# A fused dilation, state-space and convolution kernel: the scans begin with zero, ScalarE puts the kept state into their input, the extras sit in other slots

## The reference

```python
x = x + _L0_conv_ref(_gn(x))                 # 3x3 dilation (maximum)
x = x + _L1_conv_ref(_gn(x), ...)            # Mamba block on 4x4 patches
x = x + _L2_conv_ref(_gn(x), weight, bias)   # 3x3 convolution
x = x + _L3_conv_ref(_gn(x), weight, bias)   # 3x3 convolution

def step(h, inputs):                         # inside the Mamba block, token by token
    dt_t, x_t, B_t, C_t = inputs
    h = h * jnp.exp(dt_t[..., None] * A) + (dt_t * x_t)[..., None] * B_t[:, None, :]
    y = jnp.einsum('bds,bs->bd', h, C_t)
    return (h, y)
...
y = (ys + xc * D) * jax.nn.silu(z)
return jnp.einsum('bld,ed->ble', y, out_proj_w)
```

## Time and profile before

| | |
|---|---|
| three runs | 15040.47, 15045.57, 15050.49 us (median 15045.57) |
| the profiled execution | 15054.33 us, of which the span is 15052.5 us |
| busy, of the span | DVE 93%, POOL 90%, PE 84%, ACT 60% |
| scans (VectorE) | 8774.5 us with `carry`, 1202.5 us with 0.0 |
| products hc (GpSimd) | 9604.5 us |
| decays (ScalarE) | 5569.3 us |
| granted TensorE clock, mean | 0.949 |

### The profile page before, as it was taken

The page is one execution under the profiler, slowest core; times in us unless marked ns, Lnnn a source line. Parts: engine busy times, 40 slices in busy tenths (PEclk is TensorE's granted clock), DMA queues, the critical chain, the costliest instruction groups (busy, mean ns, idle before and its releaser), DMA issues.

```text
span 15052.5 us, 162697 instructions
## 1 busy us (share of the span) xinstructions
PE 12595.5 (84%) x27626; PEld 4973.4 (33%) x27626; DVE 13978.7 (93%) x12371; ACT 8975.3 (60%) x16239; POOL 13580.6 (90%) x6103
## 2 busy tenths in 40 slices
PE   4888888888888888888888888888888888888887
PEld 1333333333333333333333333333333333333332
DVE  5999999999999999999999999999999999999995
ACT  3556665566665666665656665666656666666563
POOL 5999999999999999999999999999999999999995
PEclk9999999999999999999999999999999999999998
DMA  3343443434434344443444434344343444434442
GB/s 93 105 118 116 111 123 104 125 108 112 123 106 127 106 111 121 111 124 104 113 121 110 123 106 121 113 112 122 105 129 105 109 123 111 122 107 113 121 109 81
DMA packets 1258399, 1701.57 MB, mean 113 GB/s; under 512 B 402204, under 2 KB 551140, under 8 KB 1257124
## 3 DMA queue, kind: packets, MB, share of 16 engines
q1 hardware_dynamic: 1257220, 1689.56, 40.4%
HBM read 1525.54 MB, written 124.13 MB: 110 GB/s over the span
## 4 chain that ended last, share of the span: by engine, by line
PE 33%; DVE 29%; issue 21%; POOL 9%; ACT 4%; DVEq 1%; DMA 1%; SPq 1%; POOLq 0%; ACTq 0%
PE y_ps L1026 18%; DVE h L1192 16%; DVE u_in L1176 10%; POOL hc L659 7%; PE side_ps L1037 2%; PE side_ps L1041 2%; PE b_ps L1077 2%; PE proj_ps L980 2%; POOL u_in L636 2%; PE y_ps L1023 2%; PE proj_ps L1002 2%; PE side_ps L1012 1%; PE side_ps L1045 1%; DVE vmax L1155 1%; DVE stats L1124 1%
## 5 line engine op out<-in xcount | busy, mean ns | idle before, releaser
L659 POOL TENSOR_TENSOR hc<-h,c_sb 128x1024 f32<-128x1024 f32 x4096 | 9604.5, 2358 | 952.5 <-DVE h L1192 816.6
L1192 DVE TENSOR_TENSOR_SCAN h<-a_ps,carry,u_in 128x512 f32<-128x512 f32 x7168 | 8774.5, 1264 | 367.0 <-ACT a_ps L792 196.1
L1026 PE MATMUL y_ps<-hc,ident 128*128 128x512 f32 x16400 | 8183.7, 629 | 446.3 <-POOL hc L659 440.0
L792 ACT ACTIVATE a_ps<-dt,a_neg 128x512 f32<-128x512 f32 x8192 | 5569.3, 688 | 4634.2 <-DVE h L1192 4604.4
L1026 PEld LDWEIGHTS y_ps<-hc,ident 128*128 128x128 f32 x16400 | 3191.3, 200 | 3985.2 <-issue 3065.3
L1176 DVE TENSOR_TENSOR u_in<-dtx,b_ps 128x1024 f32<-128x1024 f32 x2816 | 3368.2, 1196 | 228.0 <-PE b_ps L1077 186.4
L636 POOL TENSOR_TENSOR u_in<-dtx,b_sb 128x1024 f32<-128x1024 f32 x1281 | 3020.9, 2358 | 0.1
L1077 PE MATMUL b_ps<-b_parts,select 96*128 96x512 bf16 x2816 | 1123.9, 399 | 1639.7 <-DVE u_in L1176 1594.1
L1077 PEld LDWEIGHTS b_ps<-b_parts,select 96*128 96x128 bf16 x2816 | 278.5, 99 | 3169.7 <-DVE u_in L1176 2599.2
L1192 DVE TENSOR_TENSOR_SCAN h<-a_ps,u_in 128x512 f32<-128x512 f32 x1024 | 1202.5, 1204 | 69.0 <-POOL hc L659 55.8
L980 PE MATMUL proj_ps<-u_ln,w_x 128*128 128x512 f32 x2064 | 971.8, 593 | 4.6 <-ACT u_ln L744 3.7
(11 more groups left out here) (100 smaller groups left out, 7224.3 us busy)
## 6 DMA issues: line engine op xcount, KB each, us to landing
c_sb<-bc_dram SPq DMA_DIRECT2D x4100, 256.0 KB, 3.2
b_sb<-bc_dram SPq DMA_DIRECT2D x1283, 256.0 KB, 3.2
raw<-x SPq DMA_DIRECT2D x68, 512.0 KB
x_dram<-vmax SPq DMA_DIRECT2D x68, 512.0 KB, 4.6
z<-x_dram SPq DMA_DIRECT2D x68, 512.0 KB, 8.8
out<-raw SPq DMA_DIRECT2D x272, 128.0 KB
x_dram<-x SPq DMA_DIRECT2D x129, 256.0 KB, 4.0
x<-x_dram SPq DMA_DIRECT2D x136, 224.0 KB, 8.3
```

Of the source, the lines that this page charges most:

```text
L659: pool.tensor_tensor(hc[:, ring_at(c * S + s, HC_RING)], h[:, ring_at(c * S + s, H_RING)], c_sb[:, s // C_GROUP % C_RING, s % C_GROUP:s % ...
L792: act.activation(a_ps[:, a_slot(c * S + s, half)], dt[:, c % 2, half], ACT.Exp, scale=a_neg[:, at:at + 1]).then_inc(a_made, 1)
L1026: mm = pe.matmul(y_ps[:, half], ident[:, :], hc[:, ring_at((c * S + s) % (NC * S), HC_RING), half], start=False, stop=(s == S - 1), skip_g ...
L1192: dve.tensor_tensor_scan(h[:, r, half], a_ps[:, a_slot(c * S + s, half)], u_in[:, s % U_RING, half], start, ALU.mult, ALU.add).then_inc(h_ ...
```

## The change

1. **Scans.** All scans start with 0.0. In chunks 1 to 7 ScalarE adds the kept state's share to column 0 of the input instead: u[:, 0] += first_a * carry, one ACTIVATE on 128 x 1 for each half (`add_carry`), after the step's first decay and before its second. `first_a` is the decay of column 0 for all 32 states, made once a chunk (two ACTIVATEs of 128 x 32). The scan of such a step now waits for `carried` instead of for the input itself.
2. **Products two states ahead.** VectorE makes the input of state s + 2 at step s (before: s + 1), and TensorE broadcasts B for s + 1 at step s.
3. **GpSimd's states.** `POOL_U` keeps ten states: 22 and 25 leave, 0 and 24 come.
4. **Convolutions in five parts** in steps of their own; the strided residual product and the edge product are apart.
5. **Other slots**: the third product of the output projection 5 to 8, its copy (`residual`) 5 to 7, the store of x2 6 to 8 and with it the loads of z 7..10 to 9..12, `COPY_X` (6, 9) to (7, 10), `SILU` 13 to 14, `BASE` 10 to 12, the first softplus pieces (20, 22) to (21, 23), and two group-norm pieces by one step.

```diff
-POOL_U = [2, 6, 9, 11, 14, 17, 19, 22, 25, 27]
+POOL_U = [0, 2, 6, 9, 11, 14, 17, 19, 24, 27]
...
-CENTER, VAR, OUT = 0, 3, 5
+CENTER, VAR, OUT = 0, 3, (5, 5, 8)
...
-COPY_X, COPY_Z, SILU = (6, 9), (11, 13), 13
-GATE, STORE_X2, BASE = 2, OUT + 1, 10
+COPY_X, COPY_Z, SILU, RESIDUAL = (7, 10), (11, 13), 14, 7
+GATE, STORE_X2, BASE = 2, RESIDUAL + 1, 12
...
-PLACES = ((15, 16, 19, 22), (24, 25, 26, 27), (28, 30, S + 2, S + 2))
+PLACES = ((15, 16, 18, 19, 22), (24, 25, 26, 27, 28), (29, 30, 31, S + 1, S + 2))
...
+        first_a = sb("first_a", [P, NH, S])
...
             def make_decay(b, c, s):
                 if s == 0:
                     act.wait_ge(dt_done, chunk(b, c, NH))
+                    if c:
+                        act.wait_ge(a_made, state(b, c - 1, S - 1, NH))
+                        for half in range(NH):
+                            first = act.activation(first_a[:, half, :], a_neg[:, half * S:(half + 1) * S], ACT.Exp,
+                                                   scale=dt[:, c % 2, half, 0:1])
+                        first.then_inc(first_done, 1)
                 for half in range(NH):
...
+                    if c and half == 0:
+                        add_carry(b, c, s)
+
+            def add_carry(b, c, s):
+
+                if s == 0:
+                    act.wait_ge(first_done, first_chunk(b, c))
+                if s in DVE_U:
+                    act.wait_ge(u_made, made_by_vector(b, c, s))
+                else:
+                    act.wait_ge(pu_made, made_by_pool(b, pool_index(c, s)))
+                for half in range(NH):
+                    u0 = u_in[:, s % U_RING, half, 0:1]
+                    made = act.activation(u0, first_a[:, half, s:s + 1], ACT.Identity, bias=u0,
+                                          scale=carry[:, half, s:s + 1])
+                made.then_inc(carried, 1)
...
-                else:
+                elif part == 3:
                     pe.matmul(side_ps[:, :].rearrange("p (g w q) -> p g w q", g=CB, q=R), ident[:, :],
...
+                else:
                     pe.wait_ge(edge_in[k % 2], b * (NC * 6 * 16) + ((n * NC + k) // 2 + 1) * (6 * 16))
...
-                    pe.wait_ge(parts_in, chunk(b, c, 3 * 16))
                     for s in range(S):
-                        if s in DVE_U:
-                            k = DVE_U.index(s)
-                            pe.wait_ge(u_made, made_by_vector(b, c, s) - 1)
-                            pe.matmul(b_ps[:, :], select[:, k * P:(k + 1) * P], b_parts[:, c % 2, :],
-                                      start=True, stop=True).then_inc(b_cast, 1)
+                        broadcast_b(b, c + (s + 1) // S, (s + 1) % S)
                         sum_states(b, *behind(c, s, LAG))
...
-                    if s in DVE_U:
+                    if c:
+                        dve.wait_ge(carried, carried_state(b, c, s))
+                    elif s in DVE_U:
...
-                start = carry[:, half, s:s + 1] if c else 0.0
-                dve.tensor_tensor_scan(h[:, r, half], a_ps[:, a_slot(c * S + s, half)], u_in[:, s % U_RING, half], start,
+                dve.tensor_tensor_scan(h[:, r, half], a_ps[:, a_slot(c * S + s, half)], u_in[:, s % U_RING, half], 0.0,
                                        ALU.mult, ALU.add).then_inc(h_done, 1)
...
-                        if (s + 1 < S or c + 1 < NC) and (s + 1) % S in DVE_U:
-                            make_u(b, *behind(c, s, -1))
+                        if (s + 2 < S or c + 1 < NC) and (s + 2) % S in DVE_U:
+                            make_u(b, *behind(c, s, -2))
```

More of the change, by code:

```diff
@@ L84 @@
         CONV_AT[n, k] = [c * S + s for s in PLACES[place]]
-MEAN_AT = {"joint": (0, 23), "z1": (3, 29), "x1": (6, 24)}
-VAR_AT = {"joint": (0, 26), "z1": (4, 0), "x1": (6, 27)}
+MEAN_AT = {"joint": (0, 23), "z1": (3, 30), "x1": (6, 24)}
+VAR_AT = {"joint": (0, 26), "z1": (4, 1), "x1": (6, 27)}
 DIL_SLOTS, ADD_DILATED, STORE_ROWS = (6, 9, 11, 13, 15), 18, 21
@@ L105, in tensor_extras @@
 def tensor_extras(c, s):
-    at_state = {("center", c): [CENTER], ("var", c): [VAR], ("out", c): [OUT, OUT, OUT], ("xproj", c): XPROJ}
+    at_state = {("center", c): [CENTER], ("var", c): [VAR], ("out", c): OUT, ("xproj", c): XPROJ}
     for half in range(NH):
@@ L123, in n_parts @@
 def n_parts(use):
-    return {"x": TAPS, "conv": 4, "conv_last": 4, "out": NH + 1, "out_last": NH + 1, "xproj": NH}.get(use[0], 1)
+    return {"x": TAPS, "conv": 5, "conv_last": 5, "out": NH + 1, "out_last": NH + 1, "xproj": NH}.get(use[0], 1)
 def bank_of(use):
@@ L278, in build @@
         kept = sem("carry_kept")
+        first_done = sem("first_decays")
+        carried = sem("carry_in_first_input")
         hc_done = sem("hc_done")
@@ L338, in kept_state, with carried_state, first_chunk @@
             return b * ((NC - 1) * S) + (c * S + s + 1)
+        def carried_state(b, c, s):
+            return b * ((NC - 1) * S) + (c - 1) * S + s + 1
+        def first_chunk(b, c):
+            return b * (NC - 1) + c
         def behind(c, s, n):
@@ L918, in _ @@
                             normalise_band(b + 1, c - 1)
-                        if s == OUT:
+                        if s == RESIDUAL:
                             residual(b, ("out", c))
@@ L1046, in convolve, with broadcast_b @@
                               start=False, stop=True, skip_group_check=True).then_inc(side_filled, 1)
+            def broadcast_b(b, c, s):
+                if s == 0:
+                    pe.wait_ge(parts_in, chunk(b, c, 3 * 16))
+                if s in DVE_U:
+                    k = DVE_U.index(s)
+                    pe.wait_ge(u_made, made_by_vector(b, c, s) - 1)
+                    pe.matmul(b_ps[:, :], select[:, k * P:(k + 1) * P], b_parts[:, c % 2, :],
+                              start=True, stop=True).then_inc(b_cast, 1)
             def extra(b, part, use):
@@ L1229, in _ @@
             with dve.Fori(0, B) as b:
-                if 0 in DVE_U:
-                    make_u(b, 0, 0)
+                for s in range(2):
+                    if s in DVE_U:
+                        make_u(b, 0, s)
                 for c in range(NC):
```

3 lines of the change are left out of this document (2 added, 1 removed).

## The result

Median 14,914.0 us of 4 runs (14,910.7 to 14,917.7), against 15,048.0 us of the kernel before (15,040.5 to 15,065.2): ratio 0.991, 95% interval 0.9894 to 0.9925. The kernel is 134 us faster, where 400 were forecast. The time lies 14 us above the top of the range, and inside the band of the rival "GpSimd takes over".

The account below looks back on a forecast made before the run. VectorE was taken as the fullest engine, GpSimd 23 us an image behind. Terms -430 + 80 - 80 - 60 + 30 + 60 = -400 us gave 14,645 us, 2.7% faster, range 14,420 to 14,900.

Parts of the forecast that it names:

- GpSimd takes over: Rival: the saving becomes VectorE's waits for GpSimd's `hc`, half of it eaten; 14,750 to 14,950 us, chance 0.17.
- scans: VectorE's 7168 scans starting with zero instead of `carry` take 60 ns less each: -430 us.
- two engines at the same level: VectorE and GpSimd become level in work, so any hold-up of either reaches the other: +60 us, ends 0 and +430.
- products two ahead: VectorE's products keep number and length and neither add nor remove a TensorE wait: 0, up to +80 us.
- additions: ScalarE's one-column ACTIVATEs lengthen VectorE's wait behind the silus by 0.7 us a chunk: +80 us, ends 0 and +250.
- GpSimd's states: Moving inputs 22 and 25 to 24 and 0 takes back half of 165 us of `hc` waits: -80 us, ends 0 and -165.
- other slots: Separated convolution and output projection products take back a third of the 186.4 us of broadcast waits: -60 us, ends +40 and -190.
- the load of z: Loads issued two steps later land 1.9 us after VectorE wants them, in 16 images: +30 us, ends 0 and +100.
- waits for ScalarE above 400 us: Sign that the forecast is wrong: VectorE's waits for ScalarE exceed 400 us in total.
- ScalarE becomes the chain: Rival: additions between the decays hold up scan pairs, 0.56 us per uncovered step; slower, above 15,076 us, chance 0.07.
- The places pay more: Rival: nearly all mid-chunk `hc` and broadcast waits go and coupling costs nothing; below 14,500 us, chance 0.14.
- The 60 ns do not come: Rival: the shorter scan belongs to chunk 0, not the zero operand; about 15,020 us, chance 0.04.

Follow-up runs that it names:

- E8: E2 with all scans starting from 0.0 and nothing added, so the kept state's share is left out; 14,690.5 us, ratio 0.9760.
- E2: Kernel before with the new tables alone (GpSimd's states, slots, five convolution parts), scans starting from the kept column, products one state ahead; 14,815.5 us, ratio 0.9846.
- E3: Changed kernel without the 7168 additions, ScalarE still waiting for the input and signalling; kept state's share left out; 14,774.2 us, ratio 0.9819.
- E11: E2 with VectorE's statistics of z two steps later; 14,744.5 us, ratio 0.9794.
- E14: E11 with GpSimd's ten states as in the kernel before; 14,753.3 us, ratio 0.9800.
- E9: E2 with products and broadcasts two states ahead, scans still starting from the kept column, no additions; 14,958.1 us, ratio 0.9936.
- E20: E11 with nine GpSimd states, state 0 going to VectorE; 14,643.0 us, ratio 0.9728.
- E16: E8 with nine GpSimd states, state 0 going to VectorE; kept state's share left out; 14,500.8 us, ratio 0.9633.
- E19: Changed kernel with nine GpSimd states, state 0 going to VectorE; 14,758.8 us, ratio 0.9804.
- E1: Changed kernel's new code (zero starts, additions, two states ahead) with every table as in the kernel before; 14,986.5 us, ratio 0.9961.
- E12: Changed kernel with products one state ahead, z statistics two steps later, additions before both decays for GpSimd's inputs, behind both for VectorE's; 15,042.1 us, ratio 0.9993.

## Why the prediction was wrong, step by step

| step of the prediction | forecast | measured | by |
|---|---|---|---|
| scans, with "two engines at the same level" | -430 + 60 | -125 | E8 less E2 |
| products two ahead, with ScalarE's stop for the input and the first decays | 0 | +84 | E3 less E8 |
| additions | +80 | +140 | changed less E3 |
| GpSimd's states | -80 | -9 | E11 less E14 |
| other slots, and the load of z | -60 + 30 | -226 | E2 less before, without the row above |
| sum | -400 | -136 | |

The rows follow one chain, before, E2, E8, E3, changed, so they add up by themselves. In another order they differ: two ahead costs 143 on E2, and E3 less E9, which has the scans' saving on top of it, is -184.

To see where the time lies, VectorE's idle time can be summed by the step in which it falls (us in the whole run, counted by the order of the scans in each trace):

| where VectorE is idle | before | E2 | E14 | E20 | E8 | E16 | E9 | E3 | changed | E19 |
|---|---|---|---|---|---|---|---|---|---|---|
| first six steps of an image | 79 | 120 | 70 | 73 | 128 | 79 | 132 | 146 | 145 | 114 |
| steps 0 and 2 of all other chunks | 95 | 233 | 36 | 36 | 313 | 59 | 238 | 272 | 253 | 51 |
| behind the silus, for ScalarE | 127 | 18 | 18 | 18 | 27 | 27 | 72 | 81 | 178 | 174 |
| steps 8, 10 and 23, for the broadcast | 0 | 0 | 11 | 0 | 0 | 0 | 100 | 111 | 110 | 116 |

**The step that failed is "Two engines at the same level": +60 forecast, about 305 measured** (430 less 125; 246 by E3 less E9). Its ends, 0 and +430, held the value; the choice near the low end was wrong. The argument was that GpSimd's idle time could fall from 70 us an image to about 45, since most of it is waiting for scans. From E2 to E8 it fell from 1241.6 to 1135.0 us in the run, less than 7 an image, and not 27: its waits for scans fell by 142 us, those for the load of `c_sb` rose by 54 (35.9 to 89.7). VectorE's waits for `hc` rose by 159 us, and they lie at fixed steps: 90 of it at steps 0 and 2 of chunks 1 to 7, 59 at steps 22 to 27. So the step had it wrong that idle time of GpSimd anywhere can give way; a busy share of 91% is an average over such places. A ring of three `h` does not seem to carry slack from the one place to the other; no run has a longer ring.

**The level of the busy times does not explain it by itself.** In E2 VectorE has 390 us of work more than GpSimd (13,953.6 and 13,563.5), and the 377 that E8 takes off fit in. E16, E19 and E20 look like the proof that GpSimd's load is the bound: 285 us of work off GpSimd and 120 more on VectorE, and 190 us are gained (E16). But the state that they move is 0, whose input GpSimd makes at step 28, shortly ahead of a chunk's first steps. The table has the whole gain there: 303 us of idle time in its first two rows from E8 to E16, of 315 in all, and 233 of 254 from the changed kernel to E19. E14, with GpSimd's ten old states, has as little idle time in these rows as E20 with nine, but pays at steps 22 to 27, 92 us for `hc` and 94 at step 22 for the decays, and ends where E11 does. So GpSimd's tenth input costs 100 to 110 us in either of the two placings tried, each time at the steps next to it, and more where the scans are short (190). A third placing, or nine states with another one left out, would tell load from place; neither was run.

**GpSimd was not the whole of it.** With nine states, zero starts may be worth some 210 us (E16's 14,501 against an estimate of 14,643 + 71 = 14,714 for E20 with z as in E16): half of 430, not all. The waits for the broadcast (129.6 us) and the decays (102.8) are higher in E16 than in E20 (81.8 and 30.1), so TensorE and ScalarE take their part. How much each takes was not separated.

**"Products two states ahead: 0" was wrong in kind.** The step asked only whether the product meets its own wait for TensorE. It did not ask beside which extras the products stand once they come a step earlier. In the kernels of the table with the longer lead (E9, E3, changed, E19) VectorE waits 100 to 116 us for the broadcast at steps 8, 10 and 23, and in none of the others more than 11; behind the silus it waits 54 us more (E2 to E9, and E8 to E3), since the product beside them, on which the prediction's low end for the silus stood, has left step 15. The seam between two images adds little to VectorE's idle time, 12 us from E2 to E9. GpSimd's wait for TensorE there comes mainly with state 0 and not with the lead: its waits for the sums in the whole run are 65.2 us in E14, 112.3 in E2 and 144.8 in E9. The lead costs 84 us in this kernel and 143 in E9, whose scans are the longer ones. The table suggests why (at steps 0 and 2 and elsewhere E8 already waits where E2 does not), but no run separates it. The granted clock was also a little lower in E9 (0.944, E2 0.953); its part was not separated.

**"Additions: 80" had the mechanism and the place.** The instruction is 373 ns as in the earlier trace rows, ScalarE's busy time is 10,914 us (10,900 to 11,000 forecast), and the silus' wait grew by 0.5 us in chunk 5 and 0.8 in chunk 3 (0.7 forecast). Behind the silus VectorE waits 97 us more with the additions than without (E3 81, changed 178): that is the term, at 80. What was missing is the rest of the 140: the additions also wait for GpSimd's inputs (133.8 us, 210 times), and other extras lose their cover, which the prediction had in its high end of 250. The mark "waits for ScalarE above 400 us" was just passed: 306.5 + 104.5 = 411.

The Trainium skill (Perfetto Trace Analysis, Optimizing Scalar/DVE Operations) says that with VectorE saturated it may make sense to move some work to ScalarE. By its busy share ScalarE had room, 60% before and 73% after, and yet E3 puts the price at 140 us: most of it lies behind the silus, where an in-order queue had none. The Trainium skill (ScalarE: Activation LUTs, What ACT_TABLE_LOAD costs) gives about 93 ns for each pointer operand; the rows here agree, 191 ns without one and 372 with two.

**"GpSimd's states" and "the other slots" erred in opposite directions.** The waits for `hc` at steps 22 and 27, 178 us in the run before, are 2 us in E2, but others came, 59 us at steps 0 and 2 and longer ones at the image's start (the longest 7.8 us in E11, 4.1 in E14, which has the old states): state 0 is now made by GpSimd in front of the last `hc` of the chunk before. The slots alone (E14: the separated convolution products, the later silu, the later third output product and the rest) took 92 us of the broadcast's waits, 86 of those for `hc`, 60 of the sums' and 58 of the decays', not a third of 186 from one of them. Which slot gave what was not taken apart. This term, 196 us better than forecast with the load of z, hid most of the error of the failed step: that part was luck, and with the forecast -30 in its place the changed kernel would have been slower than before.

**The rivals.** "GpSimd takes over" held the time, and half its mechanism: the waits for `hc` rise by 159 us in E8, but in the changed kernel they are shorter than before, and what E19 gives back stands under the names of ScalarE and of the gate's sums as well. "ScalarE becomes the chain" is E1 in part (608.5 us of waits) and E12 wholly. "The places pay more" was right on the places and is E2. "The 60 ns do not come" is out: 8192 scans at 1205 ns.

## What to carry to other kernels

A saving on the fullest engine is worth neither its own length nor the distance in busy time to the next engine: 430 us off an engine that led by 23 us in 918 (398 in the whole run) were worth 125. What it is worth is decided at the steps where the engines wait for each other. One input moved away from such a step, at the fullest engine's cost, was worth 101 to 190 us each time. Where a cut needs help from another engine (an earlier product, an in-order stop in a third queue), list beside which extras the help stands in every queue, step by step; a busy share says nothing of it. And measure a bundle in halves: here the half that was thought small brought 235 us, the main idea cost 99 of it back.

## What the runs showed that was not expected

- ScalarE's 128x1 additions, 0.28 us apart and 2.3 ms in all on an engine that is idle for a quarter of the time, cost 140 us, 20 ns for each.
- Two states of lead in place of one, with the same instructions, cost 143 us (E9): the products came to stand at steps where TensorE and ScalarE have extras.
- One input of GpSimd's in 32 states, that of state 0, is behind 230 to 300 us of VectorE's idle time, at the first steps of the chunks.
- VectorE waits 3.7 us in an image for the load of z in the changed kernel (2.9 in E2), where landing times gave 1.9.
